# Graph attention layers: the order of the row broadcast in the load queue, and the value split moved from VectorE to GpSimd

## The chip, the cores and the metric

The kernel runs on one core of one Trainium2 chip. The metric is the device time of one execution in microseconds (us). The kernel before takes 2317.75 us, the median of three runs (2316.82 to 2319.7).

## What is computed

Two graph layers over 8192 nodes with 128 features, each with a residual. `adj` is an 8192 x 8192 0/1 matrix. The change touches the first layer:

```
h = relu(layernorm(x));  wh = h @ W;  wh1 = wh @ a[:128];  wh2 = wh @ a[128:]
e = wh1 + wh2.T;  e = where(e > 0, e, 0.2 * e);  e = where(adj > 0, e, -9e15)
x = x + elu(softmax(e, axis=-1) @ wh)
# second layer, untouched by the change
h = relu(layernorm(x))
att = softmax(where(adj > 0, cosine(h @ Wk.T, h @ Wq.T), -9e15), axis=1)
x = x + 0.5 * (att @ h) + 0.5 * h
```

## The kernel before

Nodes lie in 64 tiles of 128 partitions. A head stage (the first 50 us) normalises x, transposes it, makes `wh` with its two products in `v_buf`, and from them the factors of the first layer: `f_col` and `th_col` for each source node, and a row of 8192 factors that goes to HBM as `a_rows`.

The first layer then runs over 8 chunks of 1024 destination nodes. Each chunk has 32 units of two source tiles. A unit passes through one of 8 slots of `ring`, each of 128 x 2048 words:
- SyncE (SP) issues the load of 1 MB of `adj` (L266), after the slot's last user, TensorE, has counted up `s_used`.
- ScalarE (ACT) turns the integers into 0.0 or 1.0 in place (Sign, L464).
- VectorE (DVE) makes the attention weights with two SCALAR_TENSOR_TENSOR (L781), each with two tensors in SBUF as inputs: the broadcast row factors `r_ring` and the mask. It counts up `s_p`.
- TensorE (PE) runs 48 matmuls of 129 columns (L985) into one of two sets of accumulators, and counts up `s_used`.

A weight is one 32-bit word that holds two halves of 16 bits, high and low; the values in `v_buf` are split likewise. Each chunk ends on TensorE with 16 matmuls (L1002). The epilogue of chunk c (quotient, elu, residual, layer norm, split of h) is laid into chunk c+1, at given units of VectorE's and ScalarE's order of work.

`r_ring` has two halves: one chunk's row factors, broadcast to all partitions. The row of chunk c+1 is loaded (L282) during chunk c, into the half that chunk c-1 read. SP therefore waits until VectorE has done all of chunk c-1 (`s_p >= 32 * c`, L302). In the SP queue this wait and the broadcast stand ahead of the loads of chunk c's first 8 units (`group(0)`, L305). The first chunk has no `group(0)`, since its first 8 loads are issued in the head stage, and no such wait. The last chunk loads no row and has no such wait.

In the first chunk the values in `v_buf` are also scaled and split, in place, in 16 groups of four source tiles (128 x 516 elements). VectorE multiplies by `f_col` into `vz_ring`, which has two places (`value_scaled`, L707). ScalarE writes the high half (`value_high`, L408). VectorE subtracts to get the low half (`value_low`, L713). The first two groups are done ahead of the chunk's first unit, the others between the units, one VectorE operation after each unit. TensorE waits for the group's low half every second unit (L977). ScalarE's `value_high(q)` stands behind the Sign of unit 2q-3. GpSimd (POOL) is idle from the head stage on.

After the last chunk, the second layer runs to the end of the kernel.

Of the kernel before, what the change touches and what calls it, by code (L numbers as in the profile page):

```python
# [21 lines left out]
ALU = mybir.AluOpType  # L22
# [3 lines left out]
N, D, P = 8192, 128, 128  # L26
T = N // P
# [14 lines left out]
VW = D + 2  # L42
# [11 lines left out]
ZT = 4  # L54
# [8 lines left out]
def graph_layers(nc, x, adj, w, wt, a, wqk, out):  # L63
    ctx = ExitStack()
    with ctx:
        def sb(name, shape, dt=F32):
            return ctx.enter_context(nc.sbuf_tensor(name, shape, dt))

        def sem(name):
            return ctx.enter_context(nc.semaphore(name))  # L70
# [18 lines left out]
        f_col = sb("f_col", [P, T])  # L89
# [16 lines left out]
        v0 = v_buf[:, :].rearrange("p (t c) -> p t c", c=VW)  # L106
        v2 = v_buf[:, :].bitcast(F16)
        v2_tiles = v2.rearrange("p (t c) -> p t c", c=2 * VW)
# [6 lines left out]
        vz_ring = scratch[:, 2 * C0:2 * C0 + 2 * ZT * (D + 1)].rearrange("p (r t c) -> p r t c", r=2, t=ZT)  # L115
# [34 lines left out]
        s_exp0 = sem("factors_ready")  # L150
# [7 lines left out]
        s_vz = sem("values_scaled")  # L158
        s_vh = sem("values_high")
        s_vl = sem("values_low")  # L160
# [56 lines left out]
        def slot(k, dt=F32):  # L217

            return ring[:, k, :].bitcast(dt) if dt != F32 else ring[:, k, :]
# [28 lines left out]
        @block.sync  # L248
        def _(sp):
            def load_x(i):  # L250
                q = slice(X_GROUPS[i] * IW, X_GROUPS[i + 1] * IW)
                sp.dma_start(xs[:, q], x[:, q]).then_inc(s_x[i], 16)

            load_x(0)
            load_x(1)
            sp.dma_start(w_ext[:, 0:D], w).then_inc(s_w, 16)
            sp.dma_start(wt_sb[:, :], wt).then_inc(s_w, 16)
            sp.dma_start(a_sb[:, :], a).then_inc(s_w, 16)
            sp.dma_start(wqk_sb[:, :], wqk).then_inc(s_w, 16)
            for i in range(2, len(X_GROUPS) - 1):  # L260
                load_x(i)

            adj_lanes = adj.rearrange("b j p n -> p b j n")

            def load0(c, j, k):
                sp.dma_start(slot(k, I32).rearrange("p (b j n) -> p b j n", b=2, j=1),  # L266
                             adj_lanes[:, bass.ds(2 * c, 2), bass.ds(j, 1), :]).then_inc(s_adj[k], 16)

            def load1(i, j, k):
                sp.dma_start(adj_ring[:, k, :].rearrange("p (b j n) -> p b j n", b=1, j=2),  # L270
                             adj_lanes[:, bass.ds(i, 1), bass.ds(2 * j, 2), :]).then_inc(s_adj[k], 16)

            for k in range(RING0):
                load0(0, k, k)
            sp.wait_ge(s_word, 2)
            sp.dma_start(a_rows[:, :], row_word).then_inc(s_aw, 16)
            sp.wait_ge(s_aw, 16)
            a_flat = a_rows.rearrange("t p -> (t p)")

            def load_r(c, par):  # L280
                row = a_flat[bass.ds(c * C0, C0)].rearrange("(o n) -> o n", o=1)
                sp.dma_start(r_ring[:, par, :], row.to_broadcast([P, C0])).then_inc(s_rin[par], 16)  # L282

            load_r(0, 0)

            def load_h(g, r):
                sp.dma_start(h_ring[:, r, :], h_dram[:, bass.ds(g * IW, IW)]).then_inc(s_hm[r], 16)

            def chunk(c, par):
                first = isinstance(c, int) and c == 0  # L290
                last = isinstance(c, int) and c == NC0 - 1

                def group(g):
                    for k in range(RING0):

                        sp.wait_ge(s_used, U0 * c + RING0 * (g - 1) + k + 1)
                        load0(c, RING0 * g + k, k)

                if not last:
                    if not first:  # L300

                        sp.wait_ge(s_p, U0 * c)  # L302
                    load_r(c + 1, 1 - par)
                if not first:
                    group(0)  # L305
                with sp.Fori(0, G0 - 2) as h:
                    group(h + 1)
                if last:

                    sp.wait_ge(s_hw, 16 * (NC0 - 1))  # L310
                    load_h(0, 0)
                    load_h(1, 1)
                group(G0 - 1)

            chunks0(sp, chunk)

            for k in range(RING):
                sp.wait_ge(s_used, NC0 * U0 - RING0 + k + 1)
                load1(0, k, k)
            with sp.Fori(0, NI // 2 - 2) as gg:  # L320
                for r in range(2):
                    sp.wait_ge(s_ht, 2 * gg + r + 1)
                    load_h(2 * gg + r + 2, r)
            sp.wait_ge(s_hw, 16 * NC0)
            for r in range(2):
                sp.wait_ge(s_ht, NI - 3 + r)
                load_h(NI - 2 + r, r)

            def chunk1(i, par):
                first = isinstance(i, int) and i == 0  # L330

                def group(g):
                    for k in range(RING):
                        sp.wait_ge(s_m, RING * (G1 * i + g - 1) + k + 1)
                        load1(i, RING * g + k, k)

                if not first:
                    group(0)
                with sp.Fori(0, G1 - 1) as h:
                    group(h + 1)  # L340

            chunks1(sp, chunk1)


        @block.gpsimd
        def _(pool):
            nc.gpsimd.memset(ident[:, :], 0.0).then_inc(s_ident, 1)
            pool.wait_ge(s_ident, 1)
            nc.gpsimd.affine_select(out=ident[:, :], in_=ident[:, :], compare_op=ALU.not_equal, fill=1.0,
                                    base=0, pattern=[[-1, P]], channel_multiplier=1).then_inc(s_ident, 1)  # L350
            nc.gpsimd.memset(empty_w[:, :], EMPTY).then_inc(s_const, 1)
            nc.gpsimd.memset(u_buf[:, :, D:D + 2], 1.0).then_inc(s_const, 1)
            pool.wait_ge(s_ab, 5)
            nc.gpsimd.partition_all_reduce(ab_top[:, :], ab_max[:, :], P, bass.bass_isa.ReduceOp.max).then_inc(s_top, 1)


        @block.scalar
# [230 lines left out]
        def _(dve):  # L588
            V = nc.vector
# [61 lines left out]
            for g in range(TG - 2):  # L651
                q = g // 4 + 1
# [47 lines left out]
            dve.wait_ge(s_word, 4)  # L700
            dve.wait_ge(s_exp0, 2)

            def value_scaled(q):
                if q >= 2:
                    dve.wait_ge(s_vl, q - 1)
                f4 = f_col[:, ZT * q:ZT * q + ZT].unsqueeze(2).to_broadcast([P, ZT, D + 1])
                V.tensor_tensor(vz_ring[:, q % 2, :, :], v0[:, ZT * q:ZT * q + ZT, 0:D + 1], f4,  # L707
                                ALU.mult).then_inc(s_vz, 1)

            def value_low(q):  # L710
                dve.wait_ge(s_vh, q + 1)
                tiles = v2_tiles[:, ZT * q:ZT * q + ZT, :]
                V.tensor_tensor(tiles[:, :, VW:VW + D + 1], vz_ring[:, q % 2, :, :], tiles[:, :, 0:D + 1],  # L713
                                ALU.subtract).then_inc(s_vl, 1)

            def epilogue(c, par):

                at = lambda step: len(EPI0) * c + EPI0.index(step) + 1
# [42 lines left out]
            def chunk(c, par):  # L761
                first = isinstance(c, int) and c == 0
                if first:
                    parts = {2 * q - 4: (lambda q=q: value_scaled(q)) for q in range(2, T // ZT)}
                    parts |= {2 * q - 3: (lambda q=q: value_low(q)) for q in range(2, T // ZT)}
                    value_scaled(0)
                    value_scaled(1)
                    value_low(0)
                    value_low(1)
                else:  # L770
                    parts = dict(zip((3, 7, 10, 11, 15, 19), epilogue(c - 1, 1 - par)))
                dve.wait_ge(s_rin[par], 8 * c + 16 - 8 * par)
                dve.nop(nofuse=True)
                for u in range(U0):
                    k = u % RING0
                    n = U0 * c + u
                    dve.wait_ge(s_sg, n + 1)
                    dve.nop(nofuse=True)
                    for jj in range(2):
                        half = words0(k)[:, :, jj, :]  # L780
                        ins = V.scalar_tensor_tensor(half, r_ring[:, par, :].rearrange("p (b n) -> p b n", b=2),  # L781
                                                     th_word[:, 2 * u + jj:2 * u + jj + 1], half, ALU.max, ALU.mult)
                    ins.then_inc(s_p, 1)
                    if u in parts:
                        parts[u]()
# [344 lines left out]
```

## Time and profile before

| | |
|---|---|
| median of 3 runs | 2317.75 us |
| the profiled execution's own time | 2315.02 us |
| its span (first to last instruction) | 2313.2 us |
| mean granted TensorE clock | 0.983 |
| TensorE matmul busy | 2203.3 us, 95% |
| VectorE busy | 1981.7 us, 86% |
| ScalarE busy | 1633.0 us, 71% |
| GpSimd busy | 1.4 us, 9 instructions |

The span is what the trace covers; the execution's own time is 1.8 us more. Busy shares are means over the whole kernel. The first layer takes the time from about 55 to 842 us of the span. A granted clock of 1.00 is TensorE's level of 2.4 GHz and 0.50 its level of 1.2 GHz.

### The profile page before, as it was taken

To read this page: it belongs to the slowest core of one execution; us is meant where nothing else is said; L and a number is where in the kernel's file an instruction comes from. 1 tells how busy PE (TensorE), PEld (TensorE's weight loads), DVE (VectorE), ACT (ScalarE), POOL (GpSimd) and SP (SyncE) were. 2 spreads that over 40 slices of the span, in tenths; PEclk is the share of its full clock that TensorE was granted. 3 is DMA by queue.
4 is the path that set the end of the run, shared out by engine and by line. 5 is a ranking of instruction groups with operands and counts; after the bars stand their busy time and mean duration, and the time that the engine had idled before them with its cause. 6 is when DMAs were issued, how large, how long until landed. Compare 5 with 4: busy or idle time off the path is not lost.

```text
span 2313.2 us, 69259 instructions
## 1 busy us (share of the span) xinstructions
PE 2203.3 (95%) x28293; PEld 1814.4 (78%) x28293; DVE 1981.7 (86%) x1685; ACT 1633.0 (71%) x1423; POOL 1.4 (0%) x9
## 2 busy tenths in 40 slices
PE   4989999999989988999999999999999999999999
PEld 4989999999989986777767767767767767767777
DVE  7989798797979979888888888888888878888887
ACT  5768667686767757777767767767777767767776
POOL 0000000000000000000000000000000000000000
PEclk9999999999999999999999999999999999999999
DMA  6879889898989952656656656656656656656653
GB/s 241 327 275 409 323 326 403 324 398 328 379 350 392 380 204 74 213 196 210 213 183 214 214 183 213 212 185 214 208 188 211 208 175 212 214 183 214 210 194 119
DMA packets 153497, 573.55 MB, mean 248 GB/s; under 512 B 9888, under 2 KB 10336, under 8 KB 152928
## 3 DMA queue, kind: packets, MB, share of 16 engines
q1 hardware_dynamic: 144096, 549.78, 65.4%
q10 hardware_dynamic: 9216, 20.98, 2.3%
q8 instruction: 156, 2.56, 0.5%
q14 instruction: 29, 0.24, 0.0%
HBM read 558.11 MB, written 12.62 MB: 247 GB/s over the span
## 4 chain that ended last, share of the span: by engine, by line
PE 73%; DVE 11%; issue 8%; DMA 5%; ACT 3%; DVEq 0%; SPq 0%; ACTq 0%; POOL 0%; POOLq 0%
PE bank L1069 30%; PE bank L1052 29%; PE bank L985 13%; DVE ring L781 8%; DMA ring<-adj 5%; ACT ring L464 1%; DVE stats L742 0%; DVE hl_buf L806 0%; ACT hl_buf L440 0%; DVE norm L795 0%; ACT hl_buf L418 0%; DVE hl_buf L733 0%; PE bank L1013 0%; SPq L266 0%; DVE v_buf L813 0%
## 5 line engine op out<-in xcount | busy, mean ns | idle before, releaser
L528 ACT ACTIVATE ring<-bank 128x1024 f32<-128x1024 f32 x512 | 524.2, 1024 | 383.9 <-PE bank L1052 383.7
L985 PE MATMUL bank<-v_buf,ring 128*128 128x129 f16 (+1 forms) x12288 | 731.5, 222 | 47.5 <-DVE ring L781 47.1
L1069 PEld LDWEIGHTS bank<-u_buf,hl_buf 128*128 128x128 f16 x12288 | 721.8, 97 | 60.4 <-issue 0.5
L985 PEld LDWEIGHTS bank<-v_buf,ring 128*128 128x128 f16 x12288 | 724.7, 99 | 54.3 <-DVE ring L781 30.1
L839 DVE SCALAR_TENSOR_TENSOR ring<-ring 128x2048 f32<-128x2048 int32 x256 | 586.6, 2291 | 202.7 <-ACT ring L528 202.7
L1069 PE MATMUL bank<-u_buf,hl_buf 128*128 (+2 forms) x12288 | 742.4, 220 | 0.2 <-DVE hl_buf L844 0.2
L1052 PE MATMUL bank<-v_buf,q_buf 128*128 (+1 forms) x3072 | 710.5, 381 | 21.4 <-issue 19.1
L781 DVE SCALAR_TENSOR_TENSOR ring<-r_ring,th_word,ring 128x1024 f32<-128x1024 f32 x512 | 621.6, 1278 | 87.0 <-ACT ring L464 86.0
L844 DVE TENSOR_TENSOR hl_buf<-ring,hl_buf 128x2048 f16<-128x2048 f32 x256 | 584.5, 2283 | 0.0
L464 ACT ACTIVATE ring<-ring 128x2048 f32<-128x2048 int32 x256 | 481.4, 1910 | 132.8 <-DMA ring<-adj 129.0
L1052 PEld LDWEIGHTS bank<-v_buf,q_buf 128*128 (+1 forms) x3072 | 291.6, 98 | 328.9 <-issue 29.2
L534 ACT ACTIVATE hl_buf<-ring 128x2048 f16<-128x2048 f32 x256 | 487.0, 1902 | 0.6 <-DVE ring L839 0.6
L1013 PE MATMUL bank<-wqk_sb,hl_buf 128*128 128x256 f32 x128 | 34.1, 413 | 10.1 <-DVE hl_buf L806 9.7
L1013 PEld LDWEIGHTS bank<-wqk_sb,hl_buf 128*128 128x128 f32 x128 | 24.6, 203 | 16.3 <-ACT hl_buf L470 7.6
L440 ACT ACTIVATE hl_buf<-q_buf,nbias,rstd 128x128 f32 (+1 forms) x64 | 25.9, 483 | 13.0 <-DVE nbias L610 13.0
L918 PE MATMUL bank<-ident,hl_buf 128*128 128x128 f32 x128 | 21.3, 296 | 10.0 <-DVE hl_buf L619 9.9
L464 ACT ACT_TABLE_LOAD x3 | 3.8, 1283 | 37.3 <-DMA ring<-adj 37.3
L408 ACT ACTIVATE v_buf<-hl_buf 128x516 f16<-128x516 f32 x16 | 10.2, 642 | 27.2 <-DVE hl_buf L707 27.2
L918 PEld LDWEIGHTS bank<-ident,hl_buf 128*128 128x128 f32 x128 | 16.2, 151 | 13.8 <-DVE hl_buf L619 7.9
L418 ACT ACTIVATE hl_buf<-bank,den 128x128 f32<-128x128 f32 x64 | 17.3, 379 | 12.6 <-DVE den L724 12.6
L1024 PE MATMUL bank<-ident,hl_buf 128*128 128x128 f32 x128 | 18.6, 291 | 5.7 <-DVE v_buf L813 5.7
L543 ACT ACTIVATE r_ring<-bank,den 128x128 f32<-128x128 f32 x64 | 18.2, 373 | 6.7 <-DVE den L861 6.7
(102 smaller groups left out, 428.7 us busy)
## 6 DMA issues: line engine op xcount, KB each, us to landing
ring<-adj SPq DMA_DIRECT2D x512, 1024.0 KB, 5.8
r_ring<-a_rows SPq DMA_DIRECT2D x8, 512.0 KB, 4.2
x_dram<-q_buf ACTq DMA_DIRECT2D x8, 512.0 KB, 7.3
h_dram<-hl_buf ACTq DMA_DIRECT2D x8, 512.0 KB, 7.0
hl_buf<-h_dram SPq DMA_DIRECT2D x16, 256.0 KB, 2.7
r_ring<-x_dram ACTq DMA_DIRECT2D x16, 256.0 KB, 3.8
r_ring<-h_dram ACTq DMA_DIRECT2D x16, 256.0 KB, 4.0
out<-r_ring ACTq DMA_DIRECT2D x16, 256.0 KB, 3.7
```

Source lines behind the costliest of these rows:

```text
L440: ins = nc.scalar.activation(h_buf[:, it * P:(it + 1) * P], xs[:, bass.ds(c * C0 + it * P, P)], ACT.Relu, bias=nbias[:, it:it + 1], scale= ...
L464: nc.scalar.activation(slot(k), slot(k, I32), ACT.Sign).then_inc(s_sg, 1)
L528: nc.scalar.activation(p_ring[:, k, hf * 1024:(hf + 1) * 1024], bank[:, 2 * hf:2 * hf + 2, :].rearrange("p b n -> p (b n)"), ACT.Exp, scal ...
L534: nc.scalar.activation(hl_buf[:, 0, k, :], p_ring[:, k, :], ACT.Copy).then_inc(s_ph, 1)
L781: ins = V.scalar_tensor_tensor(half, r_ring[:, par, :].rearrange("p (b n) -> p b n", b=2), th_word[:, 2 * u + jj:2 * u + jj + 1], half, AL ...
L839: V.scalar_tensor_tensor(p_ring[:, k, :], adj_ring[:, k, :], 0.0, p_ring[:, k, :], ALU.is_gt, ALU.mult).then_inc(s_m, 1)
L844: V.tensor_tensor(hl_buf[:, 1, k, :], p_ring[:, k, :], hl_buf[:, 0, k, :], ALU.subtract).then_inc(s_pl, 1)
L918: ins = nc.tensor.transpose(dst[:, f], src[:, f], ident[:, :])
L985: ins = mm(acc0(par, it), weights0(k, ps)[:, it // 4, jj, f], v2[:, bass.ds((2 * j + us) * VW, D + 1)], start=start and (ps, us) == (0, 0) ...
L1013: ins = mm(qk_banks(r)[:, k * 2 * D:(k + 1) * 2 * D], ht_ring[:, r, k * P:(k + 1) * P], wqk_sb[:, :], start=True, stop=True)
L1052: ins = mm(bank[:, 2 * hf + m, :], q_buf[:, qs, bass.ds(j * P, P)], k_buf[:, ks, bass.ds(i * IW, IW)], start=(x == 0), stop=(x == 2))
L1069: ins = mm(o, hl_buf[:, ps, k, f], v.rearrange("p o c -> p (o c)"), start=head and m == 0 and it % 2 == 0 and (ps, us) == (0, 0), stop=tai ...
```

## The change

Two things are edited. In the SP queue, `group(0)` of a chunk is issued before the wait for `s_p` and the broadcast of the next chunk's row. And `value_scaled` and `value_low` of all 16 groups are removed from VectorE's order and issued on GpSimd, in the order scaled(0), scaled(1), low(0), scaled(2), low(1) and so on, behind a wait for the factors (`s_exp0`). `value_high` stays on ScalarE where it was.

```diff
@@ SP queue, first layer's chunk
+                if not first:
+                    group(0)
                 if not last:
                     if not first:
-
                         sp.wait_ge(s_p, U0 * c)
                     load_r(c + 1, 1 - par)
-                if not first:
-                    group(0)
                 with sp.Fori(0, G0 - 2) as h:
                     group(h + 1)
@@ GpSimd
+            def value_scaled(q):
+                if q >= 2:
+                    pool.wait_ge(s_vl, q - 1)
+                f4 = f_col[:, ZT * q:ZT * q + ZT].unsqueeze(2).to_broadcast([P, ZT, D + 1])
+                nc.gpsimd.tensor_tensor(vz_ring[:, q % 2, :, :], v0[:, ZT * q:ZT * q + ZT, 0:D + 1], f4,
+                                ALU.mult).then_inc(s_vz, 1)
+
+            def value_low(q):
+                pool.wait_ge(s_vh, q + 1)
+                tiles = v2_tiles[:, ZT * q:ZT * q + ZT, :]
+                nc.gpsimd.tensor_tensor(tiles[:, :, VW:VW + D + 1], vz_ring[:, q % 2, :, :], tiles[:, :, 0:D + 1],
+                                ALU.subtract).then_inc(s_vl, 1)
+
+            pool.wait_ge(s_exp0, 2)
+            for q in range(T // ZT + 1):
+                if q < T // ZT:
+                    value_scaled(q)
+                if q:
+                    value_low(q - 1)
@@ VectorE (value_scaled and value_low, the same two operations, are removed)
                 if first:
-                    parts = {2 * q - 4: (lambda q=q: value_scaled(q)) for q in range(2, T // ZT)}
-                    parts |= {2 * q - 3: (lambda q=q: value_low(q)) for q in range(2, T // ZT)}
-                    value_scaled(0)
-                    value_scaled(1)
-                    value_low(0)
-                    value_low(1)
+                    parts = {}
```

## Rows read from the trace of the kernel before

**Rows 1.** The page: busy time by engine, and the chain that ended last by engine.
```profile
PE 2203.3 (95%) x28293; PEld 1814.4 (78%) x28293; DVE 1981.7 (86%) x1685; ACT 1633.0 (71%) x1423; POOL 1.4 (0%) x9
...
PE 73%; DVE 11%; issue 8%; DMA 5%; ACT 3%; DVEq 0%; SPq 0%; ACTq 0%; POOL 0%; POOLq 0%
```
**Rows 2.** Waits, whole span: waiter, releaser, us in total, times, longest us.
```profile
ACT ring L464 <- DMA ring<-adj: 129.0, 129, 15.0
DVE ring L781 <- ACT ring L464: 86.0, 27, 11.0
PE bank L985 <- DVE ring L781: 47.1, 15, 9.8
```
**Rows 3.** Timeline of PE: start us, us, engine, line, count, idle before.
```profile
57.55 95.13 PE L985 MATMUL bank<-v_buf,ring 128*128 128x129 f16 x1536 [9.84 <-DVE ring L781]
152.52 2.00 PE L1002 MATMUL bank<-v_sum,empty_w 128*128 128x129 f32 x16
162.08 91.35 PE L985 MATMUL bank<-v_buf,ring 128*128 128x129 f16 x1536 [7.55 <-DVE ring L781]
...
692.34 56.94 PE L985 MATMUL bank<-v_buf,ring 128*128 x960 [2.05 <-DVE ring L781]
749.12 2.00 PE L1002 MATMUL bank<-v_sum,empty_w 128*128 128x129 f32 x16
750.96 66.28 PE L985 MATMUL bank<-v_buf,ring 128*128 128x129 f16 x1152
...
817.95 22.18 PE L985 MATMUL bank<-v_buf,ring 128*128 128x129 f16 x384
```
**Rows 4.** Timeline of all engines at the border from chunk 0 to chunk 1.
```profile
138.88 9.65 DVE L781 SCALAR_TENSOR_TENSOR ring<-r_ring,th_word,ring 128x1024 f32<-128x1024 f32 x8
...
148.72 0.35 SPq L282 DMA_DIRECT2D r_ring<-a_rows  x1
149.37 68.53 SPq L266 DMA_DIRECT2D ring<-adj  x27
...
159.54 9.66 DVE L781 SCALAR_TENSOR_TENSOR ring<-r_ring,th_word,ring 128x1024 f32<-128x1024 f32 x8 [11.00 <-ACT ring L464]
```
**Rows 5.** Timeline of SP from chunk 6 on.
```profile
642.85 152.90 SPq L266 DMA_DIRECT2D ring<-adj  x56
```
**Rows 6.** Timeline in chunk 0: VectorE's start, then one group of values.
```profile
49.34 1.30 DVE L707 TENSOR_TENSOR hl_buf<-v_buf,f_col 128x516 f32<-128x516 f32 x2
...
54.92 1.28 DVE L781 SCALAR_TENSOR_TENSOR ring<-r_ring,th_word,ring 128x1024 f32<-128x1024 f32 x1 [2.87 <-ACT ring L464]
...
69.31 0.69 DVE L707 TENSOR_TENSOR hl_buf<-v_buf,f_col 128x516 f32<-128x516 f32 x1
69.92 2.47 DVE L781 SCALAR_TENSOR_TENSOR ring<-r_ring,th_word,ring 128x1024 f32<-128x1024 f32 x2
70.04 0.64 ACT L408 ACTIVATE v_buf<-hl_buf 128x516 f16<-128x516 f32 x1 [1.76 <-DVE hl_buf L707]
70.58 3.70 ACT L464 ACTIVATE ring<-ring 128x2048 f32<-128x2048 int32 x2
72.31 0.69 DVE L713 TENSOR_TENSOR v_buf<-hl_buf,v_buf 128x516 f16<-128x516 f32 x1
```
**Rows 7.** Groups of instructions on POOL: line, shapes, count, busy us, mean ns.
```profile
L349 POOL TENSOR_SCALAR_AFFINE_SELECT ident<-ident 128x128 f32<-128x128 f32 x1 | 0.3, 283 | 9.6 <-issue 9.6
L347 POOL MEMSET ident<- 128x128 f32 x1 | 0.2, 205 | 0.3 <-POOLq L1123 0.3
```
**Rows 8.** Stretches: length, busy us (instructions) of PE, PEld, DVE, ACT, POOL; clock, DMA share, GB/s.
```profile
57.50:70.00 12.50, 12.45 (x179) 12.48 (x180) 12.50 (x14) 8.48 (x6) 0.00 (x0) 0.81 0.50 172
...
162.00:168.00 6.00, 5.92 (x55) 5.93 (x56) 6.00 (x7) 4.69 (x3) 0.00 (x0) 0.50 1.03 412
...
692.50:697.50 5.00, 5.00 (x61) 5.00 (x61) 5.00 (x5) 4.68 (x3) 0.00 (x0) 0.66 1.02 406
...
751.00:840.00 89.00, 89.00 (x1547) 88.99 (x1544) 75.00 (x80) 61.05 (x51) 0.00 (x0) 1.00 0.95 367
```

More of the change, by code:

```diff
@@ L701, in _ @@
             dve.wait_ge(s_exp0, 2)
[L703 to L714, printed above, removed]
             def epilogue(c, par):
```

## The prediction

> **What bounds the kernel now.** I read the page's busy times and chain first. TensorE is busy for 95% and makes 73% of the chain [rows 1], so a change pays only where TensorE stands still or runs at its low clock. The waits say where that is: in the first layer TensorE waited 47.1 us for VectorE's weights, in 15 waits; VectorE waited 86.0 us for ScalarE, and ScalarE 129.0 us for loads [rows 2]. It is a chain of three waits behind the load of `adj`. The timeline of TensorE gives the place: chunk 0's closing matmuls end at 154.5 and chunk 1 starts at 162.08, after 7.55 us of idleness; but chunk 7 starts 1.84 us after the start of chunk 6's closing matmuls (749.12 to 750.96), with no wait [rows 3]. Chunk 7 differs from the six before it in the queue: it has no broadcast and no wait for `s_p` ahead of its first loads. At the first border VectorE's last weights end at 148.53, the broadcast goes out at 148.72 and the first load of chunk 1 at 149.37, and VectorE resumes at 159.54 after 11.00 us [rows 4]. From chunk 6 on SP issues 56 loads in one unbroken row [rows 5]. So at six borders (0 to 1 up to 5 to 6) the ring of eight slots runs dry, because loads whose slots were long free stand behind a wait for VectorE's last unit.
>
> **Part 1, the loads ahead of the broadcast.** It removes the wait from in front of eight loads, at six borders. No instruction is added. I price it with chunk 7, which already runs this way. Its unit matmuls take 66.28 + 22.18 = 88.46 us (2.76 a unit) and its tail 1.84, so a chunk is 90.3 us [rows 3]. Chunks 1 to 6 took 750.96 - 162.08 = 588.9 us; six at 90.3 are 541.8. That is 47.1 us; the border 0 to 1, 7.6 us, comes on top. Inside the 47.1 lie the idle borders, small stalls after them because the pipe is dry when the epilogue comes, and the low clock: in 162 to 168 it was 0.50 and only 55 matmuls ran [rows 8], where 2.76 a unit would give 104.
>
> What hides the rest: VectorE has 75.0 busy us in the 89.0 of chunk 7, its epilogue included, and the DMA share there is 0.95 at 1.00 clock [rows 8], so the loads can just keep pace with TensorE. The broadcast that is passed over is 512 KB, half of a load. It now goes out when TensorE's last unit has freed the eighth slot, where the `s_p` wait is already met, and about 90 us before VectorE needs it; it puts the loads of `group(1)` back by about half a load's 2.5 us (1.05 MB at 412 GB/s [rows 8]), under a ring of eight units. I take 0 for it (between 0 and 1.3 us in each of six chunks, 8 us at most).
>
> **Part 2, what leaves VectorE.** In chunk 0 VectorE alternates two weights (2.47 us) with one 0.69 us value operation and has no idle time: 3.0 us a unit [rows 6], while TensorE needs 2.76. If nothing else happened, chunk 0 would fall to TensorE's pace: from 57.55, 88.46 us of units, 2.2 for the low clock at its start (179 matmuls in 12.5 us at 0.81 [rows 8] against 217 at 57.6 ns, 38 x 57.6 ns) and 1.84 of tail, so chunk 1 would start at 150.05 and not at 162.08: 12.0 us earlier, of which 7.6 are the border already named.
>
> **Part 2, what arrives on GpSimd.** 32 operations of 128x516 with two inputs. The trace shows none. The nearest rows are an AFFINE_SELECT over 128 columns at 283 ns, and a MEMSET over 128 at 205 ns [rows 7]. Times 516/128 that is 1.14 and 0.83 us for one input or none; VectorE's own 0.69 us [rows 6] is the floor, and 2 x 1.14 = 2.3 the ceiling for two inputs. I take 1.14, from the row nearest to an operation that reads and writes. Two operations are 2.3 us for a pair of units that TensorE needs 5.5 us for, so GpSimd's own speed does not bind at this value; at the ceiling, 4.6 us, only barely.
>
> The Trainium skill ("GPSIMD Engine Reference", section 3.1) gives 4497 ns for a two-input operation over 2048 columns; by length this would be 1.13 us here, an estimate of that page which no row here shows, and the sum would not move.
>
> What may bind is that both engines now read SBUF with two-input operations at the same time. No row of before has POOL beside VectorE in this stage: 0.00 in every stretch [rows 8]. The bounds are nothing at all, and all of GpSimd's time laid end to end with VectorE's. I take the second as likeliest: every weight operation of the chunk is of the two-input kind, VectorE issues them without a gap, so there is no room between them in which 27 long reads could pass unseen. The sum: five of the 32 operations (5 x 1.14 = 5.7 us) fit between 49.34, when VectorE started them before, and 54.92, when VectorE's first weights start behind the row broadcast [rows 6]. The other 27 take 30.8 us. VectorE's 64 operations no longer overlap at their ends, so 64 x 1.28 = 81.9 us. VectorE ends at 54.92 + 81.9 + 30.8 = 167.6 (148.53 before); one unit (2.76) and the tail later, chunk 1 starts at 172.2, which is 10.1 us later than before. I add 1.5 us because VectorE then has a lead of only one unit when chunk 1's epilogue work comes. Chunk 7 then starts at 172.2 + 541.8 + 1.5 = 715.5, not 750.96: 35.4 us earlier. From there on nothing is edited.
>
> The Trainium skill ("SBUF — State Buffer", section "Who interferes with whom") says that a VectorE instruction with two SBUF inputs and a GpSimd instruction that reads SBUF exclude each other for a whole instruction. By that rule the end-to-end case holds and moving work between these two engines buys nothing; without it the time is that of the first rival. The trace can't say.
>
> The waits that the change adds are on GpSimd, with nothing behind them but the next value operation; but ScalarE's `value_high(q)` waits for GpSimd in the middle of the Signs, and TensorE for the low halves. At 1.14 us these are met in time. The profiled execution took 2315.0 us, so the sum gives 2279.6; the median of the runs is 2.7 higher, so 2282 us.
>
> **The rivals.**
> - *The engines do not disturb each other.* For it: nothing in the trace shows a shared resource. Against it: two-input reads on both. Chunk 1 starts at 150.05, chunk 7 at 691.9: 59.1 us saved, 2259 us.
> - *VectorE keeps GpSimd out until its own work runs dry.* VectorE issues back to back, so GpSimd gets its turn only when ScalarE, waiting in `value_high`, has no Sign left to give. Then four units cost 8 x 1.28 + 4 x 1.14 and an exposed 0.64 + 1.9 on ScalarE [rows 6]: 17.4 us. Seven such rounds and four first units: 131.7 us, VectorE ends at 186.6, 19 later than in my sum: 2301 us. With every pair of units fully in series (5.1 + 2.3 + 2.5 = 9.9 us, 14 times) it is 2318. Against it: the two would have to be served unfairly.
> - *The other side: a GpSimd operation is far longer than its width suggests.* Its place is chunk 0, its price 27 us for each us of its length, and it decides from 2.46 us, where the 35.4 are gone (35.4 / 27 = 1.3 above 1.14). At 3.0 us the change costs 15 us: 2332. For it: no row has a two-input operation or a 16-bit one beside 32-bit ones on this engine. Against it: both rows at 1.6 to 2.2 ns a column [rows 7]. TensorE would then idle over 2 us in each unit, and such a gap was enough for the clock to be 0.66 over the 5 us after the wait of 2.05 us that ended at 692.34 [rows 3, 8]; since a unit at 0.50 takes 6.0 / 55 x 48 = 5.2 us, the two prices do not add but meet.
> - *The reordering does not bring the loads forward,* because DMA binds as soon as the wait is gone. The share of 0.95 [rows 8] leaves 5%. Then only chunk 0's loss stays: about 2328.
>
> **How the numbers follow.** The forecast (end to end, 2282) has 0.45, no disturbance 0.20, GpSimd kept out 0.20, a long operation 0.10, no gain at the borders 0.05. A measurement of this kernel can tell 0.2%, 4.6 us, from no change. Faster takes the first three but for the far end of the third: 0.84; slower is most of the last two: 0.11; within 0.2%: 0.05. The range goes from 2255, just below the undisturbed case, to 2308, which takes in the 2301 and leaves out the rest.
>
> **What would show it.** Right for part 1: SP's loads in an unbroken row across borders, TensorE chunk to chunk in 90 us, no ScalarE wait of over 3 us for a load from chunk 1 on, granted clock 1.00 there. Right for part 2: GpSimd operations of about 1.1 us that do not lie beside VectorE's, or spans of L781 over 1.28 us in chunk 0, and chunk 1 starting at about 172. I am wrong if chunk 0 ends near 150 (no shared resource) or beyond 185, or if a chunk of 1 to 6 takes over 93 us.

## The result, and the profile after

The changed kernel takes 2279.48 us (median of four runs, 2278.02 to 2279.53), the kernel before 2317.28 us. The ratio is 0.9836, with a 95% interval of 0.9819 to 0.9853. The forecast was 2282 us. The profiled execution has a span of 2277.5 us, against 2313.2 before, and a mean granted clock of 0.989, against 0.983.

The page of the changed kernel, busy time and chain, answers to [rows 1]. TensorE's share of the chain rose from 73% to 84%, DMA's fell from 5% to 1%, and GpSimd is now busy for 56.7 us:

```profile
PE 2187.7 (96%) x28293; PEld 1801.3 (79%) x28293; DVE 1984.9 (87%) x1653; ACT 1637.4 (72%) x1423; POOL 56.7 (2%) x41
...
PE 84%; DVE 9%; issue 4%; ACT 2%; DMA 1%; DVEq 0%; POOL 0%; SPq 0%; ACTq 0%
```

VectorE lost 32 operations and its busy time did not fall (1981.7 to 1984.9 us). This is the first sign that the work moved off VectorE was paid for on VectorE; the experiments below show it.

The waits of the changed kernel, whole span, answer to [rows 2]:

```profile
ACT ring L483 <- DMA ring<-adj: 165.6, 183, 6.6
...
DVE ring L782 <- ACT ring L483: 43.4, 27, 9.5
PE bank L986 <- DVE ring L782: 30.3, 17, 15.0
```

ScalarE waits for loads more in total than before (165.6 against 129.0 us), but in more and shorter waits: the longest fell from 15.0 to 6.6 us, and TensorE's own waits for weights fell from 47.1 to 30.3 us. Of these 30.3, 15.0 are the start of the first chunk.

TensorE's timeline in the changed kernel shows every chunk. It answers to [rows 3]; the start of chunk 0 and the small stalls inside it come first:

```profile
62.42 11.04 PE L986 MATMUL bank<-v_buf,ring 128*128 128x129 f16 x144 [15.04 <-DVE ring L782]
74.61 2.92 PE L986 MATMUL bank<-v_buf,ring 128*128 128x129 f16 x48 [1.15 <-DVE ring L782]
...
133.61 30.55 PE L986 MATMUL bank<-v_buf,ring 128*128 x528 [0.28 <-DVE ring L782]
164.00 2.00 PE L1003 MATMUL bank<-v_sum,empty_w 128*128 128x129 f32 x16
165.84 88.30 PE L986 MATMUL bank<-v_buf,ring 128*128 128x129 f16 x1536
...
255.81 88.30 PE L986 MATMUL bank<-v_buf,ring 128*128 128x129 f16 x1536
343.94 2.00 PE L1003 MATMUL bank<-v_sum,empty_w 128*128 128x129 f32 x16
349.48 88.29 PE L986 MATMUL bank<-v_buf,ring 128*128 128x129 f16 x1536 [3.54 <-DVE ring L782]
...
439.45 88.30 PE L986 MATMUL bank<-v_buf,ring 128*128 128x129 f16 x1536
527.58 2.00 PE L1003 MATMUL bank<-v_sum,empty_w 128*128 128x129 f32 x16
533.77 90.74 PE L986 MATMUL bank<-v_buf,ring 128*128 128x129 f16 x1536 [4.19 <-DVE ring L782]
...
626.19 88.30 PE L986 MATMUL bank<-v_buf,ring 128*128 128x129 f16 x1536
...
716.17 66.28 PE L986 MATMUL bank<-v_buf,ring 128*128 128x129 f16 x1152
```

Three things stand out. Chunk 1 takes 89.97 us from start to start (165.84 to 255.81), close to the 90.3 us that the prediction read from chunk 7; chunks 3 and 6 take the same. Two borders still have a wait of 3.5 and 4.2 us, chunk 2 to 3 and chunk 4 to 5. And chunk 0 starts 4.9 us later than before (62.42 against 57.55), and its closing matmuls begin at 164.0, against 152.5.

SP's queue, at the first border of the changed kernel, shows the new order: the row broadcast comes after `group(0)`, and then `group(1)` waits for its slots.

```profile
67.98 96.72 SPq L266 DMA_DIRECT2D ring<-adj  x32
164.89 0.34 SPq L282 DMA_DIRECT2D r_ring<-a_rows  x1
169.01 85.66 SPq L266 DMA_DIRECT2D ring<-adj  x32
```

The prediction had no row for GpSimd beside VectorE. GpSimd's timeline in the changed kernel, from the reduction on:

```profile
46.35 0.39 POOL L353 PARTITION_ALL_REDUCE ab_top<-ab_max  x1 [44.32 <-DVE ab_max L688]
53.86 2.05 POOL L359 TENSOR_TENSOR hl_buf<-v_buf,f_col 128x516 f32<-128x516 f32 x2 [7.12 <-issue]
55.88 1.12 POOL L365 TENSOR_TENSOR v_buf<-hl_buf,v_buf 128x516 f16<-128x516 f32 x1
57.08 1.04 POOL L359 TENSOR_TENSOR hl_buf<-v_buf,f_col 128x516 f32<-128x516 f32 x1
58.08 1.13 POOL L365 TENSOR_TENSOR v_buf<-hl_buf,v_buf 128x516 f16<-128x516 f32 x1
59.29 1.91 POOL L359 TENSOR_TENSOR hl_buf<-v_buf,f_col 128x516 f32<-128x516 f32 x1
61.16 2.11 POOL L365 TENSOR_TENSOR v_buf<-hl_buf,v_buf 128x516 f16<-128x516 f32 x1
```

Alone an operation takes 1.04 or 1.13 us. From 59.29 on, once VectorE's weights run (they start at 58.49), the same operations take 1.91 and 2.11. In front of the first one are 7.12 us in which the engine waits for nothing that the view shows.

### The profile page after: what moved, and what is told of

Same layout as the page of the kernel before. It is cut to its first block, busy times and chain, and to the rows that moved or that the text cites. A ratio compares the mean times of both kernels' runs of the same rounds, so it can differ in the third digit from the quotient of the medians.

```text
span 2277.5 us, 69255 instructions
## 1 busy us (share of the span) xinstructions
PE 2187.7 (96%) x28293; PEld 1801.3 (79%) x28293; DVE 1984.9 (87%) x1653; ACT 1637.4 (72%) x1423; POOL 56.7 (2%) x41
## 4 chain that ended last, share of the span: by engine, by line
PE 84%; DVE 9%; issue 4%; ACT 2%; DMA 1%; DVEq 0%; POOL 0%; SPq 0%; ACTq 0%
PE bank L1070 31%; PE bank L1053 29%; PE bank L986 23%; DVE ring L782 6%; DMA ring<-adj 1%; DVE hl_buf L638 1%; DVE hl_buf L807 0%; PE bank L1003 0%; PE bank L1014 0%; DVE hl_buf L650 0%; DVE norm L796 0%; ACT ring L483 0%; DVE v_buf L814 0%; PE bank L933 0%; DVE q_buf L814 0%
## 5 line engine op out<-in xcount | busy, mean ns | idle before, releaser
L986 PE MATMUL bank<-v_buf,ring 128*128 128x129 f16 (+1 forms) x12288 | 714.9, 220 | 30.3 <-DVE ring L782 30.3
L986 PEld LDWEIGHTS bank<-v_buf,ring 128*128 128x128 f16 x12288 | 711.1, 98 | 33.8 <-issue 25.0
L782 DVE SCALAR_TENSOR_TENSOR ring<-r_ring,th_word,ring 128x1024 f32<-128x1024 f32 x512 | 641.3, 1324 | 44.4 <-ACT ring L483 43.4
L483 ACT ACTIVATE ring<-ring 128x2048 f32<-128x2048 int32 x256 | 486.7, 1914 | 169.5 <-DMA ring<-adj 165.6
L1014 PEld LDWEIGHTS bank<-wqk_sb,hl_buf 128*128 128x128 f32 x128 | 25.3, 207 | 16.3 <-ACT hl_buf L489 7.2
L365 POOL TENSOR_TENSOR v_buf<-hl_buf,v_buf 128x516 f16<-128x516 f32 x16 | 27.7, 1728 | 29.0 <-ACT v_buf L427 29.0
L359 POOL TENSOR_TENSOR hl_buf<-v_buf,f_col 128x516 f32<-128x516 f32 x16 | 27.9, 1744 | 8.2 <-issue 7.1
```

The source lines that it names most:

```text
L359: nc.gpsimd.tensor_tensor(vz_ring[:, q % 2, :, :], v0[:, ZT * q:ZT * q + ZT, 0:D + 1], f4, ALU.mult).then_inc(s_vz, 1)
L483: nc.scalar.activation(slot(k), slot(k, I32), ACT.Sign).then_inc(s_sg, 1)
L986: ins = mm(acc0(par, it), weights0(k, ps)[:, it // 4, jj, f], v2[:, bass.ds((2 * j + us) * VW, D + 1)], start=start and (ps, us) == (0, 0) ...
L1014: ins = mm(qk_banks(r)[:, k * 2 * D:(k + 1) * 2 * D], ht_ring[:, r, k * P:(k + 1) * P], wqk_sb[:, :], start=True, stop=True)
```

## The experiments

### The two parts alone

The order of the queue alone (the first hunk of the diff on the kernel before), and the move to GpSimd alone (the other hunks).

> Only the queue order is changed; the value operations stay on VectorE. My theory: all of the gain is the order of the loads, and the move to GpSimd costs time. Chunk 0 is as before (TensorE from 57.5, closing matmuls at 152.5), chunk 1 starts at 154.4 instead of 162.1, and chunks 1 to 6 take the 550.3 us of the changed kernel instead of 588.9: 2317 - 7.7 - 38.6 = 2271 us, 8 us below the changed kernel. Rival (the move contributes to the gain, because VectorE comes to the borders with less to do): between 2279 and 2317 us, with idle borders left.

Measured: 2268.25 us (2264.88 to 2270.35), ratio to before 0.9785 (0.9767 to 0.9804). TensorE's timeline in this kernel has chunk 0 as before and chunk 1 directly behind it:

```profile
57.31 95.14 PE L984 MATMUL bank<-v_buf,ring 128*128 128x129 f16 x1536 [9.59 <-DVE ring L780]
152.29 2.00 PE L1001 MATMUL bank<-v_sum,empty_w 128*128 128x129 f32 x16
154.13 88.30 PE L984 MATMUL bank<-v_buf,ring 128*128 128x129 f16 x1536
```

> Only the value operations are moved to GpSimd; the queue order is that of before. My theory: chunk 0 runs as in the changed kernel (TensorE starts at 62.4, closing matmuls at 164.0) and the idle 7.6 us at the border comes on top, chunk 1 at 173.6 instead of 162.1: 2317 + 11.5 = 2329 us. Rival (the move helps): 2317 us or less.

Measured: 2327.85 us (2324.92 to 2330.97), ratio 1.0045 (1.0029 to 1.0061). Chunk 0's closing matmuls came at 163.91, as expected; the border idled 5.42 us and chunk 1 started at 171.33, 2.3 us sooner than I had said; chunks 1 to 6 then took 593.2 us against 588.9 before, which gave it back.

So the parts are -48.5 us and +11.1 us, together -37.4; the change as a whole is -37.8. The theory that all of the gain is the order of the loads stands, and the move to GpSimd is a loss by itself, small but clear of the noise.

### The late start

The changed kernel, with the first two groups of values left on VectorE:

```diff
 # VectorE, ahead of the first chunk's units
+                    value_scaled(0)
+                    value_scaled(1)
+                    value_low(0)
+                    value_low(1)
 # GpSimd
-            pool.wait_ge(s_exp0, 2)
-            for q in range(T // ZT + 1):
+            pool.wait_ge(s_vl, 2)
+            for q in range(2, T // ZT + 1):
```

> The changed kernel, but the first two of the 16 groups of values are scaled and split on VectorE as before, and GpSimd does the other 14. My theory: in the changed kernel GpSimd's first value operation starts 5.4 us after its inputs are ready, ScalarE's first Signs stand behind it, and so TensorE starts 4.9 us late; here TensorE starts at 57.5, and with 4 operations fewer beside VectorE chunk 1 starts about 5 us earlier: 2274 to 2276 us. Rival (only the contention counts; the late start is made up within the chunk): 2278 to 2280 us.

Measured: 2276.84 us (2274.93 to 2278.56); the interval of its ratio (0.9811 to 0.9845) overlaps that of the changed kernel, so by time alone this is a hint. The trace is clearer: VectorE started its weights at 55.11, TensorE at 59.04 and chunk 1 at 161.57, 4.3 us earlier than in the changed kernel. TensorE did not start at 57.5 as I had expected: GpSimd's first operations (from 53.69) now lay beside VectorE's first weights, and five of these took 9.84 us.

Where the 7.12 us come from was tried with one more edit on the changed kernel, a small GpSimd operation right behind the reduction:

```diff
+            nc.gpsimd.tensor_tensor(extra, extra, extra, ALU.mult).then_inc(s_extra, 1)
             pool.wait_ge(s_exp0, 2)
```

> The changed kernel with one multiplication over 128x8 on GpSimd directly behind the reduction over partitions, ahead of the wait for the factors. In the changed kernel the first value operation starts 7.1 us after the end of that reduction and 5.4 us after the factors. My theory (the 7 us follow the reduction itself, and are spent whether or not an instruction waits, because the first operation came 7.0 us after the reduction too where it waited until 5.4 us after it for other reasons): the extra operation lands where the first value operation was, at about 53.8, and the time stays at 2279. Rival (they begin with the first arithmetic instruction that is reached after the reduction): the extra operation brings this 1.8 us forward, the values start at about 52.1 and the time is 2278.

Measured: 2279.49 us (two runs, 2276.84 and 2282.14). The small operation came 7.09 us after the reduction and nothing moved forward, as expected. But my wording, that the time follows the reduction, fell with the next experiments. There GpSimd runs a MEMSET 13.4 us after the reduction, then its first TENSOR_TENSOR, and a gap of 7.2 us sits between these two, though the reduction is long past (kernel with 32 multiplications beside the weights, groups on POOL):

```profile
L361 POOL TENSOR_TENSOR hl_buf<-hl_buf 128x512 f32<-128x512 f32 x32 | 56.4, 1763 | 9.6 <-issue 7.2
L358 POOL MEMSET hl_buf<- 128x512 f32 x1 | 0.5, 528 | 13.4 <-DVE ring L788 13.4
```

With copies or MEMSETs in place of the multiplications there is no such gap (1.8 to 2.0 us of idleness over 32 operations). Over the five traced kernels with a TENSOR_TENSOR on GpSimd, the changed one included, the gap is 6.6 to 7.2 us. The program of these kernels has one extra instruction in front of the first TENSOR_TENSOR, and the trace records it as a pair of MODIFY_POOL_CONFIG: at 46.70 and 46.73 in the changed kernel, at the end of the reduction, and at 60.71, at the end of the MEMSET, in the kernel with the multiplications. The kernels with copies and MEMSETs have none there. The Trainium skill ("GPSIMD Engine Reference", section 2.1) states about 6 us for the load of newly needed code on this engine; the gap here is somewhat longer, and that it is such a load is inferred, not shown. What is shown: the gap comes once, before the first TENSOR_TENSOR, and starts with the end of the instruction ahead of it, whether or not the operation also waits for data. A row of before had a hint of it: 9.6 us put down to "issue" ahead of the AFFINE_SELECT [rows 7].

### What GpSimd beside VectorE costs

Three kernels with the queue order alone, VectorE's work untouched, and 32 GpSimd operations over 128x512 from the first units of chunk 0 on. Nothing in chunk 0 waits for them; only ScalarE does, once, long after they have ended:

```diff
+            pool.wait_ge(s_p, 2)
+            nc.gpsimd.memset(extra_a, 1.0).then_inc(s_extra, 1)
+            for n_extra in range(32):
+                pool.wait_ge(s_extra, n_extra + 1)
+                nc.gpsimd.tensor_tensor(extra_b, extra_a, extra_a, ALU.mult).then_inc(s_extra, 1)
+                # or: nc.gpsimd.memset(extra_b, 1.0)
+                # or: nc.gpsimd.tensor_copy(extra_b, extra_a)
```

> The kernel with the queue order alone (value operations on VectorE), and beside it GpSimd runs 32 multiplications over 128x512, two reads of SBUF each, back to back from the first unit of chunk 0 on; nobody waits for them. My theory (the engines take turns, a whole instruction each): every GpSimd operation costs VectorE about 0.8 us, as in the changed kernel; VectorE's weights take about 2 us each while it lasts, GpSimd's own 1.9 us instead of 1.0; about 26 us in chunk 0 and 2290 us in all. Rival (the loss in the changed kernel came from the chain of waits from GpSimd over ScalarE to VectorE, not from the shared reads): weights stay at 1.28 us and the time at 2268.

> As the kernel with 32 GpSimd multiplications beside the weights, but each is a MEMSET of the same 128x512 elements: GpSimd only writes. My theory (it is the reads that exclude each other): weights stay at 1.28 us, 2268 us. Rival (any GpSimd operation takes the turn): weights are longer by the length of a MEMSET each time, up to 0.8 us, and the time is 2275 us or more.

> As the kernel with 32 GpSimd multiplications beside the weights, but each is a copy of 128x512 elements: GpSimd reads once and writes. My theory (a read on GpSimd takes the turn, however many): the copies lie end to end with the weights, which are longer by less than with two inputs, since a copy is shorter: 2275 to 2285 us. Rival (only two-input operations on GpSimd disturb): 2268 us.

Measured: 2293.51 us with multiplications (2292.82 to 2294.98, three runs), 2266.47 with MEMSETs (2265.95 and 2266.99), 2278.08 with copies (2277.99 and 2278.17), against 2268.25 without. The last was measured on another chip, on which the kernel before took 2316.76 us, against 2317.40 on theirs. By operation that is 25.3 / 32 = 0.79 us, nothing, and 9.8 / 32 = 0.31 us. The start of chunk 1 in the traces gives the price in its place: 179.77, 154.79 and 166.40 us, against 154.13 without, so 25.6 / 32 = 0.80 us for a multiplication and 12.3 / 32 = 0.38 us for a copy. The start with MEMSETs is 0.7 us later, but so was the start of chunk 0 (57.98 against 57.31). The groups on VectorE in 60 to 90 us show it directly. Multiplications on GpSimd (they begin only at 67.87):

```profile
L788 DVE SCALAR_TENSOR_TENSOR ring<-r_ring,th_word,ring 128x1024 f32<-128x1024 f32 x15 | 24.8, 1692 | 0.0
```

MEMSETs on GpSimd, for which VectorE's weights keep their 1.28 us:

```profile
L788 DVE SCALAR_TENSOR_TENSOR ring<-r_ring,th_word,ring 128x1024 f32<-128x1024 f32 x21 | 26.0, 1276 | 0.0
```

Copies on GpSimd, and GpSimd's own side of it, 1326 ns for an operation that only copies:

```profile
L788 DVE SCALAR_TENSOR_TENSOR ring<-r_ring,th_word,ring 128x1024 f32<-128x1024 f32 x16 | 24.8, 1583 | 0.0
```
```profile
L361 POOL COPY hl_buf<-hl_buf 128x512 f32<-128x512 f32 x32 | 42.4, 1326 | 2.0
```

Beside a GpSimd operation that reads, one read being enough, VectorE's two-input operations take longer; beside one that only writes they do not. The rival, that the loss came from the chain of waits over ScalarE, fell: nothing in chunk 0 waits for these operations and the price of one is nearly the same. This is what the Trainium skill states ("SBUF — State Buffer", section "Who interferes with whom"): a VectorE instruction with two SBUF inputs contends with a GpSimd instruction that reads SBUF, and not with one that only writes.

### The two borders that still wait

The queue order alone, with TensorE's loop over pairs of chunks written out:

```diff
-            chunks0(pe, chunk)
+            for c in range(NC0):
+                chunk(c, c % 2)
```

> As the kernel with the queue order alone, and TensorE's loop over pairs of chunks is written out as eight chunks (same instructions, same order, no branch back between chunks 2 and 3 and between 4 and 5). In the changed kernel TensorE still stands still for 3.5 and 4.2 us at just these two borders, though VectorE had finished four units of the next chunk. My theory: the branch back to the loop's start costs this. Both waits go, and the low clock after the second: 550.3 - 541.8 = 8.5 us less than the order alone, 2262 us. Rival (a load or VectorE is late at these borders): same as the order alone, 2271 us, and the two waits stay.

Measured: 2259.87 us (2259.26 to 2260.78), ratio 0.9754 (0.9737 to 0.977), 8.4 us below the order alone. TensorE's timeline in this kernel at the border of chunks 2 and 3:

```profile
332.55 2.00 PE L1001 MATMUL bank<-v_sum,empty_w 128*128 128x129 f32 x16
334.39 88.47 PE L984 MATMUL bank<-v_buf,ring 128*128 128x129 f16 x1536
```

Both waits are gone. They were no waits for weights, though the view names VectorE as the releaser of those in the changed kernel (in other kernels of this study it says "issue"). TensorE's closing matmuls of chunk 2 end at 345.94 and it resumes at 349.48. VectorE's timeline of the changed kernel has the first four units of chunk 3 (eight operations, 1.2 us apart) between 337.07 and 346.73: three of them were done when TensorE stopped, and the fourth 2.7 us before it resumed.

```profile
337.07 9.66 DVE L782 SCALAR_TENSOR_TENSOR ring<-r_ring,th_word,ring 128x1024 f32<-128x1024 f32 x8 [1.98 <-ACT ring L483]
...
346.64 0.30 DVE L730 RECIPROCAL den<-bank 128x3 f32<-128x3 f32 x3
```

So the branch back to the loop's start costs TensorE 2.4 to 4.3 us each time (3.5 and 4.2 in the changed kernel, 4.3 and 2.4 in the one with the order alone). Why it does is open. The loop holds some 2300 matmuls; the inner loop, with 384, shows no gap.

VectorE has such a loop too. It stands still at its own branch back before chunks 3 and 5, for 5.9 and 5.7 us in the kernel above; the first of the two:

```profile
329.67 9.65 DVE L780 SCALAR_TENSOR_TENSOR ring<-r_ring,th_word,ring 128x1024 f32<-128x1024 f32 x8 [5.89 <-issue]
```

In the changed kernel, which has fewer instructions on VectorE, the same idle times are 2.0 us (the row of 337.07) and 0.7 us. TensorE's lead of some units hides most of this, but not all, as the next kernels show.

### Who should take the work instead

The kernel with TensorE's loop written out, with the scaling of the values on ScalarE (as four activations with a scale for each partition), the low halves on VectorE, nothing on GpSimd:

```diff
 # ScalarE, ahead of each value_high(q)
+                for t in range(ZT * q, ZT * q + ZT):
+                    ins = nc.scalar.activation(vz_ring[:, q % 2, t % ZT, :], v0[:, t, 0:D + 1], ACT.Copy,
+                                               scale=f_col[:, t:t + 1])
+                ins.then_inc(s_vz, 1)
```

> The kernel with the queue order and TensorE's chunk loop written out, and the scaling of the values (not the low halves) moved from VectorE to ScalarE, as four activations with a scale for each partition instead of one two-input operation; GpSimd does nothing. My theory (what an operation costs depends on the engine that takes it, and ScalarE has room): in chunk 0 ScalarE needs about 3.7 + 0.6 + 1.1 = 5.4 us and VectorE 4.8 + 0.6 = 5.4 us for two units, TensorE 5.5 instead of the 6.0 that VectorE set before; chunk 0 becomes up to 7 us shorter and the time about 2253 us. Rival (ScalarE's waits for the low halves in the middle of its Signs cost what VectorE saves): 2260 us or more.

> The kernel with the queue order and TensorE's chunk loop written out once more, on the same chip as the one with the scaling on ScalarE, so that the two can be told apart: 2260 us, as the first time.

Measured: 2254.70 us (2253.64 to 2257.68, four runs), and 2261.54 us without the move (2254.94 to 2261.66, four runs; one lay at the faster end). The medians are 6.8 us apart, but the ranges of the times overlap, and so do the intervals of the two ratios (0.9725 to 0.9766, and 0.9737 to 0.9785). The traces say where the gain lies. Chunk 0's matmuls take 89.99 us against 95.13, and chunk 1 starts at 149.88 against 154.27, 4.4 us earlier:

```profile
58.21 89.99 PE L985 MATMUL bank<-v_buf,ring 128*128 128x129 f16 x1536 [10.48 <-DVE ring L781]
148.04 2.00 PE L1002 MATMUL bank<-v_sum,empty_w 128*128 128x129 f32 x16
149.88 88.30 PE L985 MATMUL bank<-v_buf,ring 128*128 128x129 f16 x1536
```

The rest lies in chunks 1 to 6: 539.8 us here, 544.5 without the move and 541.3 in that kernel's first trace. There TensorE waited for weights inside chunks 3 and 5, behind VectorE's idle times of 6.4 and 7.3 us at its branch back. With the scaling on ScalarE these are 1.9 and 1.3 us:

```profile
321.42 9.66 DVE L781 SCALAR_TENSOR_TENSOR ring<-r_ring,th_word,ring 128x1024 f32<-128x1024 f32 x8 [1.86 <-ACT ring L474]
```

Why VectorE's branch got cheaper with fewer instructions on that engine is not shown. VectorE's weights kept their 1.27 us, and ScalarE was then busy for 87.3 of 90 us in 60 to 150, so there is no room for more there.

By its median it is the fastest kernel of the study, ratio 0.9746 to before (0.9725 to 0.9766).

## Why the prediction was right, step by step

The direction, the mechanism of both parts and the total (2282 forecast, 2279.5 measured) were right, but the closeness of the total is in part luck. Chunk 0 was forecast 6.4 us too long and chunks 1 to 6 together 7.0 us too short, and inside chunk 0 a term of 35.5 us measured 22.4 while two others had been left out or were too small. Two of the prediction's own signs also went against it: it called itself wrong if a chunk of 1 to 6 took over 93 us, and chunks 2 and 4 took 93.7 and 94.3; and it wanted no ScalarE wait of over 3 us for a load from chunk 1 on, and there were three, of 4.3, 3.6 and 6.6 us.

**The order of the loads.** Predicted: six borders without idleness, a chunk in 90.3 us, the trailing broadcast at no cost. Measured: 89.97 us from start to start in chunks 1, 3 and 6, the granted clock 1.00 in them, and the part alone gave 48.5 us. The sum had 54.7 (47.1 and 7.6). What was missing from it is the branch back in TensorE's loop: in the changed kernel 3.7 us at chunk 2 to 3, 4.35 at 4 to 5, and 2.4 more in chunk 5, which ran at clock 0.50 for its first 5 us. Chunks 1 to 6 took 550.3 us and not 543.3. The pattern was there to be read: chunk 7, my template, is not entered by a branch back.

**What leaves VectorE.** Predicted: 3.0 us a unit before, TensorE's 2.76 if nothing else happened. The kernel with the scaling on ScalarE, which takes one of the two value operations off VectorE, has chunk 0 at 89.99 / 32 = 2.81 us a unit, so this is confirmed, by other means than GpSimd.

**GpSimd's own operation.** Taken at 1.14 us from the AFFINE_SELECT row, with bounds of 0.69 and 2.3. Measured 1.04 and 1.13 when alone. The rival of a far longer operation fell.

**The shared reads.** Predicted: end to end, one by one. The mechanism holds, but its size was overstated, and this is the largest error of the sum. I charged 30.8 + (81.9 - 77.2) = 35.5 us for 27 operations, 1.31 us each, where 77.2 is 64 operations at the unbroken 1.21 [rows 4]. In the changed kernel VectorE runs 72 weights in one unbroken row of 109.32 us from 58.49; at 1.21 they would take 86.9, so 22.4 us were lost over 27 operations, 0.83 each. The kernel with 32 multiplications gives 0.79. Neither engine was kept out: with both busy in 60 to 80 us a weight takes 2012 ns and a value operation 1906 or 2107.

```profile
L782 DVE SCALAR_TENSOR_TENSOR ring<-r_ring,th_word,ring 128x1024 f32<-128x1024 f32 x12 | 23.3, 2012 | 9.5 <-ACT ring L483 9.5
```
```profile
L365 POOL TENSOR_TENSOR v_buf<-hl_buf,v_buf 128x516 f16<-128x516 f32 x5 | 10.5, 2107 | 1.2 <-ACT v_buf L427 1.2
L359 POOL TENSOR_TENSOR hl_buf<-v_buf,f_col 128x516 f32<-128x516 f32 x5 | 9.5, 1906 | 0.4
```

That they take whole turns is read from single operations, VectorE's first three weights beside GpSimd's rows above:

```profile
58.49 1.80 DVE L782 SCALAR_TENSOR_TENSOR ring<-r_ring,th_word,ring 128x1024 f32<-128x1024 f32 x1 [9.51 <-ACT ring L483]
60.21 2.06 DVE L782 SCALAR_TENSOR_TENSOR ring<-r_ring,th_word,ring 128x1024 f32<-128x1024 f32 x1
62.20 2.15 DVE L782 SCALAR_TENSOR_TENSOR ring<-r_ring,th_word,ring 128x1024 f32<-128x1024 f32 x1
```

Weights end at 60.29, 62.27 and 64.35, value operations at 59.21, 61.20 and 63.27: the ends alternate, 0.9 to 1.1 us apart. A weight and a value operation together take 2.03 us. End to end they would take 1.21 and 1.04 to 1.13, which is 2.25 to 2.34: some 0.2 to 0.3 us of each pair overlap, and my sum had let nothing overlap. What part of an operation overlaps is not shown. This is less than the exclusion for a whole instruction that the prediction took from the Trainium skill ("SBUF — State Buffer", section "Who interferes with whom"); the measurement decides.

**The start.** I let GpSimd begin at 49.34, where VectorE had begun. It began at 53.86; ScalarE's first Signs stand behind its first two operations, and VectorE started at 58.49 and not at 54.92. This term, 3.6 us, was not in the sum at all. It comes from the gap ahead of the first TENSOR_TENSOR.

**The sum again.** 172.2 forecast for the start of chunk 1; minus 13.1 for the overstated sharing, plus 3.6 for the late start, plus 3.1 because TensorE was 5.9 us behind VectorE at the end of the chunk and not one unit (VectorE's chunk ended at about 158.1, the closing matmuls began at 164.0), gives 165.8; measured 165.84. The 5.9 us come from the chunk's end: TensorE's last wait for weights ended at 133.61, and from there on, with GpSimd nearly done, VectorE made a unit in 2.45 us and TensorE took 2.78. Then +7.0 over six chunks: chunk 7 at 716.2, forecast 715.5. That puts the profiled execution at 2279.5, forecast 2279.6; the 2.7 us added for the median of the runs had no counterpart (the median is 2279.48), and they are the rest of the miss.

**The rivals.** No disturbance (2259) is refuted by the widened weights. VectorE keeping GpSimd out (2301) is refuted by the alternating ends. No gain at the borders (2328) is refuted by the kernel with the order alone; the 2328 us that it named are what the move to GpSimd alone gives.

## What to carry to other kernels

A wait in a queue of loads holds back everything behind it: put the loads whose slots are free ahead of the one that waits for another engine, and price it by a stage of the same trace that already runs without the wait. Before moving an operation off a busy engine, ask what it costs that engine where it goes: here 0.60 us of VectorE's time on VectorE itself (3.0 us a unit against 2.41), 0.8 us on GpSimd, through the turns that the two engines take, and nothing measurable on ScalarE, as long as that engine has room. Two changes in one can hide each other; the half that lost 11 us was invisible in a total that gained 38.

## What was not expected

- The first TENSOR_TENSOR on GpSimd comes 6.6 to 7.2 us after the end of the instruction ahead of it; MEMSET and copy have no such gap.
- TensorE stands still for 2.4 to 4.3 us, with its inputs ready, where its outer loop branches back, and not where its inner loop does; written out, 8.4 us are gained. VectorE idles for 5.4 to 7.3 us at its own branch back in the kernels that have the new queue order and keep both value operations there, and for 0.7 to 2.1 us in those that move them, wholly or in part.
- A GpSimd copy with one read is enough to lengthen VectorE's two-input operations, by 0.3 to 0.4 us for each copy of 128x512.
